# PNA gather stages on one core: one selection for maximum and minimum, a lifting matmul, sum units over more slots, scan rows one by one

## The reference, cut to what matters

```
xi = x @ W_pre[:Fin];  xj = x @ W_pre[Fin:]
h = xi[dst] + xj[src] + b_pre
mean = segment_sum(h, dst) / degc
mean_sq = segment_sum(h * h, dst) / degc
mx = segment_max(h, dst);  mn = segment_min(h, dst)
...
out = concatenate([x, agg, agg * amp, agg * att]) @ W_post + b_post
```

## Time and profile before

| what | us |
|---|---|
| median of 3 runs (lowest to highest) | 2619.86 (2617.08 to 2621.5) |
| span of the profiled execution | 2642.1 |
| gather stage of layer 0, from PE's first selection to DVE's last row | 919 to 1638 |
| gather stage of layer 1 | 1798 to 2509 |
| busy over the whole span: PE, DVE, POOL | 1813.7 (69%), 1755.5 (66%), 1421.5 (54%) |

### The profile page before, as it was taken

The page is one execution under the profiler, slowest core; times in us unless marked ns, Lnnn a source line. Parts: engine busy times, 40 slices in busy tenths (PEclk is TensorE's granted clock), DMA queues, the critical chain, the costliest instruction groups (busy, mean ns, idle before and its releaser), DMA issues.

```text
span 2642.1 us, 36266 instructions
## 1 busy us (share of the span) xinstructions
PE 1813.7 (69%) x12224; PEld 1202.1 (46%) x12224; DVE 1755.5 (66%) x4356; ACT 418.4 (16%) x931; POOL 1421.5 (54%) x1116
## 2 busy tenths in 40 slices
PE   0047777677688558888888851664998789886255
PEld 0024554445578425555555531441555456554133
DVE  4988888888640786656566673487666567657438
ACT  2124333343100101010110110120010101011001
POOL 2758888888040065555456575305556555646530
PEclk9988888888889888889899975786999889987567
DMA  3112222222134235555355443115555455543320
GB/s 84 54 29 90 90 77 78 78 97 93 71 130 141 75 125 183 167 175 190 127 169 202 160 151 103 50 42 170 175 179 171 154 171 186 199 144 131 133 82 25
DMA packets 148823, 327.20 MB, mean 124 GB/s; under 512 B 51084, under 2 KB 102605, under 8 KB 148315
## 3 DMA queue, kind: packets, MB, share of 16 engines
q1 hardware_dynamic: 95674, 159.39, 17.9%
q10 hardware_dynamic: 23152, 104.77, 10.9%
q0 software_dynamic: 29872, 61.49, 8.2%
HBM read 172.44 MB, written 153.12 MB: 123 GB/s over the span
## 4 chain that ended last, share of the span: by engine, by line
PE 43%; DVE 24%; issue 11%; POOL 8%; another core or an unknown queue 4%; ACT 4%; DMA 3%; SPq 1%; ACTq 0%; DVEq 0%; POOLq 0%
PE ps L1055 19%; PE ps L1138 12%; POOL scanned L988 5%; DVE scanned L1528 4%; PE ps L1068 3%; PE ps L1122 3%; ACT A L685 3%; POOL scanned L939 3%; DVE scanned L1912 2%; DVE scanned L1908 2%; PE ps L1192 2%; PE ps L1245 1%; DMA A<-counts 1%; DVE S L1507 1%
## 5 line engine op out<-in xcount | busy, mean ns | idle before, releaser
L988 POOL DMA_INDIRECT scanned<-table,rest_idx x784 | 839.3, 1070 | 849.1 <-DVE scanned L1912 347.7
L1055 PE MATMUL ps<-big,A 125*128 125x128 bf16 (+1 forms) x7500 | 764.6, 260 | 146.3 <-issue 102.5
L1055 PEld LDWEIGHTS ps<-big,A 125*128 125x128 bf16 x7500 | 629.8, 105 | 309.4 <-issue 178.2
L1138 PE MATMUL ps<-S,big 126*128 126x500 bf16 (+3 forms) x2100 | 494.0, 389 | 219.8 <-DVE accs L1860 102.1
L939 POOL TENSOR_SCALAR scanned<-scanned 128x400 bf16<-128x400 f16 x200 | 429.2, 2154 | 108.0 <-PE ps L1068 56.2
L1138 PEld LDWEIGHTS ps<-S,big 126*128 126x128 bf16 (+1 forms) x2100 | 207.2, 107 | 455.7 <-issue 152.8
L1860 DVE TENSOR_TENSOR accs<-accs,ps 128x1000 f32<-128x1000 f32 (+1 forms) x154 | 166.4, 1080 | 290.4 <-remote 179.6
L1068 PE MATMUL ps<-scanned 128*128 128x400 bf16 x1000 | 242.6, 382 | 124.2 <-DVE scanned L1528 89.0
L1908 DVE SCALAR_TENSOR_TENSOR scanned<-scanned,rest_neg 128x128 f32<-128x128 f32 x784 | 269.5, 344 | 83.4 <-DMA scanned<-table,rest_idx 73.1
L1528 DVE TENSOR_SCALAR scanned<-scanned 128x400 bf16<-128x400 f16 x800 | 316.2, 454 | 0.0
L1912 DVE SCALAR_TENSOR_TENSOR scanned<-scanned,rest_neg 128x128 f32<-128x128 f32 x784 | 269.1, 343 | 0.0
(11 more groups left out here) (306 smaller groups left out, 1431.5 us busy)
## 6 DMA issues: line engine op xcount, KB each, us to landing
rest_history<-scanned SPq DMA_DIRECT2D x112, 896.0 KB
A<-counts ACTq DMA_DIRECT2D x75, 800.0 KB
S<-picks SPq DMA_DIRECT2D x60, 640.0 KB
picks<-S ACTq DMA_DIRECT2D x25, 800.0 KB, 3.4
counts<-A ACTq DMA_DIRECT2D x25, 800.0 KB, 3.3
scanned<-table,rest_idx POOLq DMA_INDIRECT x784
scanned<-records SPq DMA_DIRECT2D x200, 7.5 KB, 1.6
table<-Y SPq DMA_DIRECT2D x10, 320.0 KB, 2.5
```

The costliest lines, as they stand in the source:

```text
L988: nc.gpsimd.indirect_dma_start(out=rows[:, w, s, :], out_offset=None, in_=tables[1 + l], in_offset=bass.IndirectOffsetOnAxis(ap=rest_idx[: ...
L1055: m = nc.tensor.matmul(acc[:, bank, 0:width], A[0:NB, slot, a, :], XS[0:NB, a, c, 0:width], start=a == 0 and c == 0, stop=a == NT - 1 and ...
L1138: m = nc.tensor.matmul(ps[:, bank + h, 0:len(blocks) * NB], XS[0:rows, a, c, 0:F], pick[0:rows, n % RING, 0:len(blocks), a % PART, 0:NB], ...
```

## The change

One `select` for each slot gives the picked rows with -ABSENT (126 rows of XS), DVE takes the maximum from it, then PE adds one matmul for each source block (`lift_absent`: weights `lift`, all zero but row NB + 1, which holds 2 * ABSENT; 128 rows of picks, into the same banks with start=False), and DVE takes the minimum from the same banks. The bank pairs 4/5 and 6/7 now alternate by slot. PE runs `select` of slot s + 1 ahead of the lift of slot s; one sum unit stands between them and the others behind. The sum units are dealt over 80 slots instead of 69. The scan rows are dealt one by one: 392 rows over 91 slots, 4 or 5 in a slot, half of them (rounded down) between `take_top` and `take_low`, the others at the slot's end. POOL waits for each row of the window two before, in place of the whole window. `fill` writes one row of XS and not two. The order of the groups, the picks' loads and the work before and after the stages are as before.

```diff
-TOP_BANK, LOW_BANK = 4, 6
+SELECT_BANKS = [4, 6]
...
-UNIT0, UNIT_SLOTS = 6, 69
+UNIT0, UNIT_SLOTS = 6, NSLOT - 11
...
-SCANNED = [range(s * WINDOWS // NSLOT, (s + 1) * WINDOWS // NSLOT) for s in range(NSLOT)]
+SCANNED = [range(s * REST // NSLOT, (s + 1) * REST // NSLOT) for s in range(NSLOT)]
...
                 for k in range(WINDOWS):
                     n, w = l * WINDOWS + k, k % 2
-                    if n > 1:
-                        pool.wait_ge(main.scan_ops, 2 * WIN * (n - 1))
                     for s in range(WIN):
+                        if n > 1:
+                            pool.wait_ge(main.scan_ops, 2 * ((n - 2) * WIN + s + 1))
                         nc.gpsimd.indirect_dma_start(
...
-            def select(l, s, bank, rows, taken, done):
-
-                blocks = GROUPS[slot_group(s)]
-                if l * NSLOT + s > 0:
-                    pe.wait_ge(taken, l * NSLOT + s)
+            def select(l, s):
+
+                n = l * NSLOT + s
+                bank, blocks = SELECT_BANKS[n % 2], GROUPS[slot_group(s)]
+                if n > 1:
+                    pe.wait_ge(lowered, n - 1)
...
                     for c in range(3):
-                        m = nc.tensor.matmul(ps[:, bank + h, 0:len(blocks) * NB], XS[0:rows, a, c, 0:F],
-                                             pick[0:rows, n % RING, 0:len(blocks), a % PART, 0:NB],
+                        m = nc.tensor.matmul(ps[:, bank + h, 0:len(blocks) * NB], XS[0:NB + 1, a, c, 0:F],
+                                             pick[0:NB + 1, part % RING, 0:len(blocks), a % PART, 0:NB],
                                              start=c == 0, stop=c == 2)
-                m.then_inc(done, 1)
+                m.then_inc(selected, 1)
+
+            def lift_absent(l, s):
+
+                n = l * NSLOT + s
+                bank, blocks = SELECT_BANKS[n % 2], GROUPS[slot_group(s)]
+                pe.wait_ge(topped, n + 1)
+                for h, a in enumerate(slot_sources(s)):
+                    part = l * NPARTS + part_of(s, a)
+                    m = nc.tensor.matmul(ps[:, bank + h, 0:len(blocks) * NB], lift[:],
+                                         pick[:, part % RING, 0:len(blocks), a % PART, 0:NB],
+                                         start=False, stop=True, skip_group_check=True)
+                m.then_inc(lifted, 1)
...
+                select(l, 0)
                 for s in range(NSLOT):
-                    select(l, s, TOP_BANK, NB + 1, topped, top_selected)
-                    select(l, s, LOW_BANK, NB + 2, lowered, low_selected)
-                    for b, q in UNITS[s]:
...
+                    if s + 1 < NSLOT:
+                        select(l, s + 1)
+                    for b, q in UNITS[s][:1]:
+                        unit(b, q)
+                    lift_absent(l, s)
+                    for b, q in UNITS[s][1:]:
+                        unit(b, q)
...
                     take_top(l, s)
+                    half = len(SCANNED[s]) // 2
+                    for i in SCANNED[s][:half]:
+                        scan_row(l, i)
                     take_low(l, s)
...
-                    for k in SCANNED[s]:
-                        window(l, k)
+                    for i in SCANNED[s][half:]:
+                        scan_row(l, i)
```

More of the change, by code:

```diff
@@ L199, in gnn_kernel @@
         ones = sb("ones", [P, P])
+        lift = sb("lift", [P, F], BF16)
         limit = sb("limit", [P, 1])
@@ L1871, in take_low @@
                 cols = len(GROUPS[g]) * NB
-                bank = LOW_BANK
-                dve.wait_ge(low_selected, n + 1)
+                bank = SELECT_BANKS[n % 2]
+                dve.wait_ge(lifted, n + 1)
                 if i == 0:
```

73 lines of the change are left out of this document (41 added, 32 removed).

## The result

The changed kernel takes 2532.31 us (median of 4 runs, 2526.32 to 2538.96), the kernel before beside it 2620.68 (2617.08 to 2622.56): a ratio of 0.966 by these medians. The ratio on record beside them is 0.9746, 95% interval 0.9693 to 0.9798; why the two differ it does not show, so the gain is 2.5 to 3.4%. Either way it is faster, and by half or less of the 174 us that the forecast of 2446 held: 88 us by the medians, 67 by the ratio.

The account below looks back on a forecast made before the run. PE was taken to bound the middle of both gather stages. Layer 0 was to go from 719 to 631 us and layer 1 from 711 to 623, 174 us off the median, giving 2446 us, with a range of 2355 to 2600.

Parts of the forecast that it names:

- POOL's price: Gather stages: POOL needs 1.35 us a row, 5.8 us a slot, below 6.8, so it is not the bound.
- The start of the stage: Slots 0 to 5: DVE waits for the first dealt row, adding 6 us in each layer.
- D: Rival: the handshake makes DVE the bound through its wait for the lift, 1.39 us a slot; 2705 us, chance 0.09.
- So PE sets the middle.: Slots 6 to 77 of each gather stage: PE, busy 493 of 570 us, sets the pace; DVE follows PE, POOL follows DVE.
- Units over 80 slots: Slots 6 to 77: 12 units and 2 turned-block uses move to the last group, 23 + 6 us less a layer.
- Selections: Slots 6 to 77: 276 fewer matmuls of 500 columns on PE, 69 us less a layer, between 63 and 76.
- The new handshake: Slots 6 to 77: PE waits for DVE's minimum, net 14 us more a layer; 5 more for slots where cover fails.
- Rows one by one: Later slots: POOL gets further ahead and fetches fewer rows in the last group, 15 us less a layer, between 0 and 30.
- The last group: From slot 78 on, where POOL is nearest the bound: 15 us less in each layer, 97 to 82 in layer 0.
- B: Rival: POOL becomes the bound without interference, the stage takes 534 us; 2261 us, chance 0.07.
- C: Rival: POOL becomes the bound because dealt scan operations slow nearly every issue to 1.41 us; 2540 us, chance 0.14.
- E: Rival: no change, because stretches with late signals stretch to fill what PE saves; 2620 us, chance 0.04.

Follow-up runs that it names:

- before_units80: The kernel before with only the sum units dealt over 80 slots instead of 69, on the disturbed machine: 2618.19 us, ratio 1.0002.
- units80_again: The kernel before with only the sum units dealt over 80 slots instead of 69, on an undisturbed machine: 2349.9 us, ratio 1.0002.
- before_rows_units80: The kernel before with rows dealt one by one and units over 80 slots, without the selection change, on an undisturbed machine: 2247.8 us, ratio 0.9597.
- before_permits: The kernel before with POOL waiting row by row while DVE still scans whole windows, on an undisturbed machine: 2332.23 us, ratio 0.9907.
- before_dealt: The kernel before with DVE's rows dealt one by one while POOL still waits for whole windows, on an undisturbed machine: 2395.8 us, ratio 1.02.
- after_again: The changed kernel run again unaltered, beside the kernel before, on an undisturbed machine: 2257.07 us, ratio 0.9598.
- windows: The changed kernel with whole windows again in DVE's scan and POOL's permits, on the disturbed machine: 2623.2 us, ratio 1.0025.

## Why the prediction was half right

*The sign, the number of matmuls and POOL's price* held. PE has about 550 matmuls of 500 columns in the middle (418 + 138) and lost 87 us of busy time there, against 69 + 29 in the sum; the selections' part of it is 46 and not 69 (205.6 to 116.9 + 42.8 us, at a clock of 0.89 and not 0.91). POOL's mean issue is 1.011 and not 1.4. The start of the stage is 6 and 1 us longer (forecast 6 and 6).

The other signs named beforehand speak against the forecast. The middle is 530 us and not near 490, with PE busy 77% of it. DVE's wait for the lift is 125 us, 1.7 a slot, above the 1 us that was to tell for D, though 87.5 of it are "remote". POOL's wait for DVE's rows is 145 us (124.2 + 21.1) and not well below 157.8. That 2532 lies inside the range of 2355 to 2600 is therefore luck and not a merit of the sum, whose terms are not what made the time.

**The step that failed is the first one: "So PE sets the middle."** With it, work taken off PE was counted as time, 98 us a layer. The runs beside the result show that such work was worth nothing there: the units alone 1.0002, the selections and the units with whole windows 1.0025, and all of the gain came with the dealt rows, which had no term in the middle.

The step was drawn from 493 busy of 570 with only 8 us of waits for DVE. The idle time on it was "issue", and I took POOL (318 busy) and DVE (367) as far from the bound by the same means. But a stall can stop all three, so it lowers each engine's share and hides who sets the pace between stalls. On the machines without them the middle is 465, PE has 445 of it and POOL 464 with its gaps. The comparison "5.8 us in a slot, below 6.8" put POOL's price against a slot's mean that had 113 / 72 = 1.6 us of the disturbance in it; the clean slot is 6.5, and POOL's price in it is 1.112 + 0.30, that is 309 x 1.41 = 436 and its waits for whole windows. That this pace between stalls is the same on the disturbed machine is inferred from the others, not measured on it. From this follow three terms:

- *Units over 80 slots*, 29 us a layer. By itself 0 on both kinds of machine (before_units80, units80_again); on the undisturbed one POOL held the same end. After the dealing 25 and 23 us there (before_rows_units80), near the 29. The size was right, the condition not seen.
- *Selections*, 69 us a layer. Worth nothing undisturbed: 429 and 426 us with the change, 423 and 426 with all else but this. The removed work turned into waits, PE's for DVE and DVE's for the lift.
- *The new handshake*, 14 + 5 us a layer. Against what PE's work alone would allow (379 of 429) it costs 50 us, against the floor of the gathers (415) still 14. The 14 counted only PE's wait for the minimum in slots with one unit. That DVE waits for the lift too (0.66 us a slot) was named as rival D, with 1.39, and called covered. The disturbed runs pay more: the lift's other place is worth 1.2% there by the medians (2502 against 2532, not run side by side), nothing on the undisturbed machine (2256 and 2257).

*Rows one by one*, 0 to 30 us a layer in the forecast, 15 taken, put down to the last group. It is all of the gain on the disturbed machine, 127 us by the medians; by the traces 57 and 64 in the two middles and 15 and 12 in the last groups, less 4 at the first start. On the undisturbed machine it is 52 us: by the traces 17 and 13 in the middles, 13 and 11 in the last groups, less 4. That it comes in the middle, where I had put no term for it, is the second miss; and it takes both halves (before_permits -22, before_dealt +42). That the disturbance costs 113 us with windows and 73 with rows is measured, and so is that 27 us of the difference in layer 0 are PE's busy time, at a higher granted clock. That DVE's bursts and POOL's late permits hinder the catching up after a stall is argued, not shown.

*The last group* shrank by 6 us a layer instead of 15. On the undisturbed machines it is 10 (81 to 71, 79 to 69).

*The rivals.* B (POOL, without interference, 2261) is near what the undisturbed machine shows, 2257, but by chance: there were no late signals there to go, and POOL is not the bound. C fell: POOL's mean issue did not rise when the scan was dealt out, it is 1.011. Undisturbed, the mean is 1.112 beside bursts of 14 and 1.013 dealt out, and the longest issue in layer 0's middle 3.94 us and 1.92, so bursts were the worse case. The Trainium skill ("SBUF — State Buffer", SBUF: two separate sides) calls the port pair that VectorE and GpSimd share an exclusive lock, held for the whole instruction, for VectorE operations with two SBUF inputs against GpSimd operations that read SBUF. The trace agrees in part: undisturbed, with whole windows, the 117 issues in layer 0's middle that meet a scan operation in their first 0.9 us take 1.37 us in the mean, the 191 others 0.96; but about half of those that meet one are no longer than 1.00. Dealt out (after_again) 214 meet one and take 1.04, the 91 others 0.95. So more issues are hit and each hit costs less, as the forecast had held against C. D's mechanism is real at half its price. E is near the truth for the selections and the units: with whole windows (windows) they give 1.0025.

In hindsight, for the undisturbed machine: before 465, less 29 for the units and less 41 for the selections on PE, 395; but the handshake holds it at 429, and the gathers would at 415. That is 36 us a layer and the ends, 2257. The 275 us from there to 2532 are 101 and 94 in the two middles and 26 in the other parts of the stages, and some 50 us lie outside the gather stages, where nothing was changed (1206 us in after, 1155 in after_again).

## What to carry to other kernels

Where a trace has stretches in which every engine stands and the idle time of the busiest one is "issue", take them out first and compare the engines' needs by the pace between them; a share of the mean hides a second engine at the bound. Two engines at the bound make each single edit look worthless (units alone 0, with the dealt rows 48 us in the two middles), so test edits in pairs. And work taken off an engine by making it answer the other one twice in a step can come back whole as waiting: here 41 us of matmuls were taken off PE in layer 0, and in the loop of maximum, lift and minimum it waited 51. And a time measured on one machine may not hold on the next: set only kernels beside each other that ran on the same one.

## What was not expected of the hardware

The same program took 2620 us on one machine and 2350 on another, 11% apart, each within 2% over 9 to 19 runs, and the same change was worth 2.5% (3.4 by the medians) on the one and 4.0% on the other, dealing the rows 4.6% and 2.2%. On the slower machines PE halts in steps of 0.70 us with nothing to wait for that the profile shows, and behind such halts its matmuls can take nearly twice as long (2.68 us for six, against 1.44) at a granted clock of 0.50. On the undisturbed machines an indirect gather's issue took 1.008 us in the mean where the f32 scan beside it came in fours and fives, and 1.112 where it came in fourteens.
